# Decoder block: half of the next query ahead of the norm's transposes, values copied by ScalarE, and two additions moved into the attentions

## The chip, the cores and the metric

One core of a Trainium2 chip runs the whole program. The metric is the device time in microseconds of one execution. TensorE (PE), VectorE (DVE), ScalarE (ACT), GpSimd (POOL) and the DMA queue that SyncE issues (SP) run side by side and wait for each other through semaphores.

## The reference

A post-norm decoder block on 4 batches of 1024 tokens of width 256, with 16 heads of width 16: a self attention with low-rank query, key and value and rotary terms, a cross attention on 154 context rows, and a mixture of 8 experts.

```python
ct_q = x @ Wd_q_w + Wd_q_b
qt_c = heads(ct_q @ Wu_q_w + Wu_q_b)
qt_r = heads(_rope(ct_q @ Wq_r_w + Wq_r_b, cos, sin))
query = qt_c + qt_r
ct_kv = x @ Wd_kv_w + Wd_kv_b
kt_c = heads(ct_kv @ Wu_k_w + Wu_k_b)
kt_r = heads(_rope(x @ Wk_r_w + Wk_r_b, cos, sin))
key = kt_c + kt_r
value = heads(ct_kv @ Wu_v_w + Wu_v_b)
...
x = _layernorm(x + attention(query, key, value) @ Wo_w + Wo_b)
x = _layernorm(x + cross_attention(x, ctx))
x = _layernorm(x + experts(x))
```

## The kernel before

The batches run one after the other: self attention, a passage, cross attention, a second passage, and so on; the experts of all batches come at the end. The order on each engine is written out by hand, and semaphores join the engines. An attention has two kinds of score products. The maxima (L1582 in the self attention, L1573 and L1576 in the cross attention) are reduced by DVE (L1122, L1117) to one negative maximum per row. POOL splits that into three bf16 parts (`split_max`, L780 to L786), PE turns it (L1624), ACT copies it (L966) and SP loads it as three more rows of the query stack (L571). The transposed scores (L1640, L1646, L1657) then go through ACT's exponential (L958) and are multiplied with the values (L1674, L1678). Heads go in 8 groups of two. In the cross attention a group has 4 units of maxima; groups 0 to 3 read the query stack in `qxs` (semaphore `s_qx[0]`), groups 4 to 7 the one in `qst` (`s_qx[1]`). Five groups of maxima run before the first transposed score. A turn of group g stands in PE's order after the maxima of group g+1, so group g+2 waits for POOL's split of group g.

float32 accuracy is kept by splitting queries and keys into three bf16 parts, and a stack of 96 rows holds six products of parts. That is done in pieces of 128x512. Piece (b, i) is of batch b: i of 0 to 3 is the query (half i // 2 of the tokens, two pieces each), 4 to 7 the key, 8 the context's key, 9 to 12 the cross query, where 9 and 10 make the stack in `qxs` and 11 and 12 the one in `qst`. A piece goes: product on PE (one matmul of 512 float32 columns shows as two records); for a query or key the rotary step `roped` on DVE, two pieces at a time (L1070 and L1073, L1078 and L1079, and L1083, which writes `full`); for a cross query ACT's bias (L918, writes `full`). Then ACT's first part (L904), POOL's difference (L762), ACT's second part (L925), POOL's third (L769). ACT and POOL work one piece ahead: the second part of a piece stands behind the first part of the next one. SP stores the three parts of a piece to DRAM (L541, `store_piece`), and when all of a stack are stored (`stored`) loads them back six times (L566, `load_stack`: 6 DMAs of 256 KB). `full` and `rest` are two buffers each in `pT`; the parts have six slots, four in `kst` and two (`lent`) in `pT`.

In the passage from self to cross attention of batch b (`rest_of_batch`), PE makes the output projection (L1773), the latents of batch b+1 (L1549 with wdq and wdkv, taken by ACT at L932), the turns of the normalised x (L1541), the four cross queries `qx`, the query and key products of b+1 (L1793, L1796, L1549 with wkr) and its values (L1803). DVE normalises (L1173), does four rotary steps and adds the bias to the values (L1186). POOL adds the bias of the cross attention's output to the residual (L826) ahead of the pieces. PSUM has 8 banks, given out in turn: a product waits until the one eight places before it is taken.

Of the kernel before, what the change touches and what calls it, by code (L numbers as in the profile page):

```python
# [26 lines left out]
ALU = mybir.AluOpType  # L27
# [34 lines left out]
OPERANDS = [("q", "D")] * 8 + [("k", "D")] * 8 + [("v", "D")] * 4  # L62
CONTEXT = [("kx", "A"), ("vx", "D"), ("vxr", "D")]
FRONT = LATENTS + OPERANDS + CONTEXT
OUT_SELF = [("o", "D")] * T + [("oT", "DA"[n % 2]) for n in range(4)] + [("y", "D")] * 4
INTO_CROSS = [("x1T", "A")] * 4 + [("qx", "A")] * 4
# [54 lines left out]
PIECES = 13  # L121
RING = 6


def slot(i):
    return (i - (i > 8)) % RING


def stored_upto(ring, i):

    return len([n for n in range(i) if n != 8 and slot(n) == ring])
# [131 lines left out]
def decoder_block(nc, a, out):  # L263
    ctx = ExitStack()
    with ctx:
# [89 lines left out]
        parts_at = [part[:, i, :, :] for i in range(RING - 2)] + [lent[:, i, :, :] for i in range(2)]  # L355
# [92 lines left out]
        s_xb = sem("residual_ready")  # L448
        s_p1 = sem("part1_ready")
# [42 lines left out]
        def parts_of(i):  # L492
            return [part_x[:, k, :] if i == 8 else parts_at[slot(i)][:, k, :] for k in range(3)]
# [5 lines left out]
        def _(sp):  # L499
# [37 lines left out]
            def store_piece(b, i, dst, cols):  # L537

                sp.wait_ge(s_p4, b * PIECES + i + 1)
                for k in range(3):  # L540
                    sp.dma_start(dst[k], parts_at[slot(i)][:, k, 0:cols]).then_inc(s_pw[slot(i)], 16)  # L541

            def store_context(b):

                wait_apart(sp, s_p4, b * PIECES + 9)
# [5 lines left out]
            def stored(b, i):  # L551

                wait_apart(sp, *[w for r in range(RING) for w in (
                    s_pw[r], 48 * (b * stored_upto(r, PIECES) + stored_upto(r, i + 1)) + START)])

# [20 lines left out]
            def store_front(b, pieces):  # L576
                for i in pieces:
                    store_piece(b, i, rows_of(q_parts if i < 4 else k_parts, i % 2, i % 4 // 2), N)

            def load_keys(b, thirds):  # L580
                if 0 in thirds:
                    stored(b, 7)
# [30 lines left out]
            def rest_of_batch(b, more):  # L613
# [4 lines left out]
                def store_cross(pieces):  # L618
                    for i in pieces:
                        mc, half = (i - 9) // 2, (i - 9) % 2  # L620
                        store_piece(b, i, [qx_parts[k, mc * P:(mc + 1) * P, half * N:(half + 1) * N]
                                           for k in range(3)], N)

                def load_cross(mc):
                    stored(b, 10 + 2 * mc)
                    load_stack(heads_of(qst, 1) if mc else qxs[:, :, :], qx_parts, mc, 0, s_qx[mc])

                if more:
                    store_cross(range(9, 13))
                    load_cross(0)  # L630

                    wait_apart(sp, s_ql[0], b * 96 + 96, s_ql[1], b * 96 + 96, s_kl[0], b * 96 + 96,
                               s_kl[1], b * 96 + 96)
                    store_front(b + 1, range(4))
                    load_cross(1)
                    stored(b + 1, 3)
                    load_stack(heads_of(qst, 0), q_parts, 0, 0, s_ql[0])
                    store_front(b + 1, range(4, 8))
                else:
                    store_cross(range(9, 11))  # L640
                    load_cross(0)
# [1368 lines left out]
```

## Time and profile before

| | |
|---|---|
| median of 3 runs | 1862.75 us (1860.33 to 1869.51) |
| the profiled execution | 1864.3 us, of which the span on the engines is 1862.4 us |
| granted clock of TensorE, mean | 0.931 |
| busy: PE, DVE, ACT, POOL | 1638.1 us, 1203.4 us, 888.1 us, 430.6 us |
| first self attention starts | 69.05 us |
| passages from self to cross attention (from the last value product's end to the first cross maxima) | about 287 to 351 us, 664 to 726 us, 1038 to 1102 us; of the last batch 1413 to 1463 us |
| the chain that ended last: PE, DVE, issue, ACT, DMA | 67%, 11%, 6%, 5%, 4% |

A timeline row has the start, the duration, the engine, the line, the operation with output and inputs, how many, and in brackets the idle time before it and what ended it. Rows "x4" that overlap in time are pipelined.

### The profile page before, as it was taken

Reading aid. Unit: us, or ns where it says so; the run is one execution under the profiler, and the core shown is the slowest. Engines: PE = TensorE matmul, PEld = TensorE weight load, DVE = VectorE, ACT = ScalarE, POOL = GpSimd, SP = SyncE. Lnnn points to the kernel's source line nnn. Section 1 sums busy time; section 2 is a strip of 40 time slices with the busy share of each in tenths; the row PEclk is TensorE's granted clock in tenths of the full one; section 3 lists DMA queues with packets and bytes.
Section 4 is the critical chain, followed back from the end, with each engine's and each line's share of the span. In section 5 each row is a group of like instructions: output and inputs, shape, how many; then the busy total and the mean of one; then the engine's idle time right before and its main releaser. Section 6 shows DMA issues by size and latency. Waiting matters only on the chain.

```text
span 1862.4 us, 27223 instructions
## 1 busy us (share of the span) xinstructions
PE 1638.1 (88%) x10046; PEld 814.2 (44%) x10046; DVE 1203.4 (65%) x2136; ACT 888.1 (48%) x1582; POOL 430.6 (23%) x543
## 2 busy tenths in 40 slices
PE   7499999798899997988999979889997698999993
PEld 3023325445233244452332445523324446888873
DVE  5577744865777759647777496477776634664443
ACT  2067774252677742526777425257774261111111
POOL 4300003501100025011000260110001401566663
PEclk9589999898899998988999989889999797999997
DMA  5800001823100017222000072220000413455594
GB/s 183 180 6 1 1 2 43 208 53 79 54 1 1 2 35 207 62 64 68 2 2 1 27 204 73 62 71 2 2 2 1 120 48 102 74 113 111 113 260 116
DMA packets 108256, 128.24 MB, mean 69 GB/s; under 512 B 17244, under 2 KB 81756, under 8 KB 108124
## 3 DMA queue, kind: packets, MB, share of 16 engines
q1 hardware_dynamic: 95836, 109.71, 21.3%
q0 software_dynamic: 12288, 16.79, 5.4%
q8 instruction: 80, 1.31, 0.3%
q14 instruction: 52, 0.43, 0.1%
HBM read 84.49 MB, written 40.79 MB: 67 GB/s over the span
## 4 chain that ended last, share of the span: by engine, by line
PE 67%; DVE 11%; issue 6%; ACT 5%; DMA 4%; POOL 2%; SPq 2%; POOLq 0%; ACTq 0%; DVEq 0%
PE banks L1674 13%; PE banks L1640 11%; PE banks L1582 10%; PE banks L1921 5%; PE banks L1934 4%; PE banks L1773 2%; PE banks L1573 2%; PE banks L1549 2%; PE banks L1576 2%; PE banks L1644 2%; PE banks L1624 2%; PE banks L1678 2%; PE banks L1684 2%; DVE z L1143 2%; PE banks L1831 2%
## 5 line engine op out<-in xcount | busy, mean ns | idle before, releaser
L958 ACT ACTIVATE pT<-banks 128x512 f32<-128x512 f32 x1184 | 645.1, 595 | 272.7 <-PE banks L1640 167.5
L1122 DVE TENSOR_REDUCE nmf<-banks 128x1 f32<-128x1024 f32 x512 | 606.0, 1221 | 183.3 <-PE banks L1582 181.9
L1640 PE MATMUL banks<-qst,kst 99*128 99x512 bf16 x1024 | 349.8, 389 | 18.8 <-DMA qst<-nmT 9.3
L1582 PE MATMUL banks<-kst,qst 96*128 96x512 bf16 x1024 | 328.0, 405 | 32.7 <-DMA kst<-k_parts 22.8
L1674 PE MATMUL banks<-pT,V 128*32 128x512 f32 x2048 | 274.5, 608 | 17.3 <-ACT oT L946 12.2
L1640 PEld LDWEIGHTS banks<-qst,kst 99*128 99x128 bf16 x1024 | 95.9, 97 | 312.6 <-ACT pT L958 187.0
L780 POOL CAST nmp<-nmf 128x16 bf16<-128x16 f32 x64 | 12.7, 198 | 833.4 <-issue 759.5
L1582 PEld LDWEIGHTS banks<-kst,qst 96*128 96x128 bf16 x1024 | 98.6, 100 | 148.9 <-DVE nmf L1122 36.8
L1117 DVE TENSOR_REDUCE nmf<-banks 128x4 f32<-128x616 f32 x128 | 99.9, 798 | 66.1 <-PE banks L1576 58.9
L1027 ACT ACTIVATE kst<-banks 128x512 f32<-128x512 f32 x64 | 38.2, 597 | 205.8 <-PE banks L1921 205.8
L966 ACT ACTIVATE nmT<-banks 6x1024 bf16<-6x1024 bf16 x64 | 64.8, 1013 | 130.3 <-PE banks L1624 129.1
L819 POOL DMA_INDIRECT acc_rows<-kst,tok_s x64 | 103.1, 1611 | 47.6 <-DMA acc_rows<-kst,tok_s 17.9
L1573 PE MATMUL banks<-maskb,identb 128*128 128x308 bf16 x256 | 81.4, 330 | 31.9 <-DVE V L1186 25.8
L1674 PEld LDWEIGHTS banks<-pT,V 128*32 128x32 f32 x2048 | 41.3, 108 | 126.9 <-ACT pT L958 126.0
L793 POOL TENSOR_TENSOR rstd<-ve,mhalf 128x4 f32<-128x4 f32 x16 | 16.3, 1020 | 330.0 <-DVE ve L1167 330.0
L1434 DVE TENSOR_SCALAR kst<-banks,gate 128x256 f32<-128x256 f32 x64 | 28.0, 479 | 95.1 <-PE banks L1934 95.1
L810 POOL DMA_INDIRECT kst<-x_rows,tok_g x64 | 65.4, 1021 | 70.8 <-issue 49.7
L1141 DVE RECIPROCAL rz<-banks 128x16 f32<-128x16 f32 x64 | 15.9, 249 | 101.7 <-PE banks L1757 101.7
L889 ACT ACTIVATE xT<-banks 128x512 f32<-128x512 f32 x40 | 22.7, 598 | 94.6 <-PE banks L1528 54.9
L1921 PE MATMUL banks<-kst,qst 128*128 128x256 f32 x256 | 60.3, 391 | 0.0
L1934 PE MATMUL banks<-qst,kst 128*128 128x256 f32 x256 | 58.4, 381 | 0.0
L1921 PE MATMUL banks<-kst,qxs 128*128 128x256 f32 x256 | 58.0, 379 | 0.3 <-issue 0.3
(200 smaller groups left out, 2296.9 us busy)
## 6 DMA issues: line engine op xcount, KB each, us to landing
qst<-q_parts SPq DMA_DIRECT2D x48, 256.0 KB, 6.3
kst<-k_parts SPq DMA_DIRECT2D x48, 256.0 KB, 4.4
qst<-in_w SPq DMA_DIRECT2D x16, 512.0 KB, 5.2
qxs<-in_w SPq DMA_DIRECT2D x16, 512.0 KB, 5.0
q_parts<-kst SPq DMA_DIRECT2D x48, 128.0 KB, 2.4
qxs<-qx_parts SPq DMA_DIRECT2D x24, 256.0 KB, 5.2
qst<-qx_parts SPq DMA_DIRECT2D x24, 256.0 KB
kst<-in_xT SPq DMA_DIRECT2D x4, 1024.0 KB, 5.0
```

The source lines that it names most:

```text
L810: pool.indirect_dma_start(xg[k][:, j, :], None, x2_rows[0:(EARLY if n < EARLY * E else B) * S, :], bass.IndirectOffsetOnAxis(tok_g[q % 2][ ...
L819: pool.indirect_dma_start(acc_rows, bass.IndirectOffsetOnAxis(tok_s[q % 2][:, k, j:j + 1], 0), yg[k][:, j, :], None, compute_op=ALU.add).t ...
L958: act.activation(pT[:, n % RING_P, :], PS[:, banks[what, n], :], ACT.Exp, scale=scale).then_inc(s_ex, 1)
L966: act.activation(nmT[:, m % 2, :], PS[0:3 * G, banks[what, n], :].bitcast(BF16), ACT.Copy).then_inc(s_ne, 1)
L1117: dve.tensor_reduce(nmf[:, m % 2, j, 4 * u:4 * u + 4].rearrange("p (a t) -> p a t", a=2), scores[:, :, 0:2 * SK].rearrange("p a (t k) -> p ...
L1122: dve.tensor_reduce(nmf[:, m % 2, j, t:t + 1], scores.rearrange("p a n -> p (a n)"), AX.X, ALU.max, negate=True).then_inc(s_smu, 1)
L1573: pe.matmul(ps[:, 0:2 * SK], identb[:, :], maskb[:, t0:t0 + 2, 0:SK], start=True, stop=False, skip_group_check=True)
L1582: ins = pe.matmul(pair[:, half, :], qst[0:KQ, h, t * P:(t + 1) * P], kst[0:KQ, h, half * N:(half + 1) * N], start=True, stop=True)
L1640: ins = pe.matmul(ps, kst[0:KM, head, kc * P:(kc + 1) * P], qst[0:KM, head, cols], start=True, stop=True)
L1674: ins = pe.matmul(av[V32 * j:V32 * (j + 1), :], Vf[:, kc, (g * G + j // HALVES) * VD:(g * G + j // HALVES) * VD + V32], pT[:, n % RING_P, ...
L1921: ins = pe.matmul(PS[:, 2 + 2 * k + f // 2, (f % 2) * CAP:(f % 2 + 1) * CAP], we1[w % WEIGHTS][:, c, f * P:(f + 1) * P], xgT[k][:, c, :], ...
L1934: ins = pe.matmul(PS[:, 6 + k, j * D:(j + 1) * D], hT[k][:, f, j * P:(j + 1) * P], we2[w % WEIGHTS][:, f, :], start=(f == 0), stop=(f == F ...
```

## The change

In the passages between two batches PE multiplies the first half of batch b+1's query ahead of the turns of the normalised x, then two of the four cross queries, then the rest of the query, the keys and values, and last the other two cross queries. The pieces get one numbering over the whole program (`PIECES`, `NUMBER`), in the order (b+1,0), (b+1,1), (b,9), (b,10), (b+1,2) to (b+1,7), (b,11), (b,12), (b+1,8); ACT, POOL and SP follow it. SP loads the stack in `qxs` behind (b,10), the first query stack of b+1 behind (b+1,5) and the second cross stack behind (b,12). The values are copied by ACT without their bias (new `values`, 4 ACTIVATE), just ahead of piece (b+1,6), and POOL adds the bias to all of them in one instruction behind the split of cross group 3 (`bias_values`, semaphore `s_vb`, for which the first product with the values waits). At the start of the program the values stand behind piece (0,7) on ACT, and the bias behind piece (0,8) on POOL. POOL's addition to the residual (`after_layernorm`) moves from ahead of the pieces to behind the split of cross group 1, in the last batch too; `mask_bias` and `residual` of b+1 move behind the splits of self groups 1 and 2.

```diff
-OPERANDS = [("q", "D")] * 8 + [("k", "D")] * 8 + [("v", "D")] * 4
+HALF_Q = [("q", "D")] * 4
+KEYS = [("k", "D")] * 8
+VALUES = [("v", "A")] * 4
...
-EACH = Plan(OUT_SELF + LATENTS + INTO_CROSS + OPERANDS, OUT_CROSS + CONTEXT + ROUTING)
-LAST = Plan(OUT_SELF + INTO_CROSS, OUT_CROSS + ROUTING)
+EACH = Plan(OUT_SELF + LATENTS + HALF_Q + TURNED + HALF_X + HALF_Q + KEYS + VALUES + HALF_X,
+            OUT_CROSS + CONTEXT + ROUTING)
+LAST = Plan(OUT_SELF + TURNED + HALF_X * 2, OUT_CROSS + ROUTING)
...
+def pieces_between(b):
+
+    if b < 0:
+        return [(0, i) for i in range(9)]
+    if b == B - 1:
+        return [(b, i) for i in range(9, 13)]
+    return ([(b + 1, 0), (b + 1, 1), (b, 9), (b, 10)] + [(b + 1, i) for i in range(2, 8)]
+            + [(b, 11), (b, 12), (b + 1, 8)])
...
+                for piece in pieces_between(b):
+                    if piece[1] == 8:
+                        continue
+                    store_piece(piece)
+                    if piece == (b, 10):
+                        stored(piece)
+                        load_stack(qxs[:, :, :], qx_parts, 0, 0, s_qx[0])
+                    elif piece == (b + 1, 5):
+                        stored((b + 1, 3))
+                        load_stack(heads_of(qst, 0), q_parts, 0, 0, s_ql[0])
+                    elif piece == (b, 12):
+                        stored(piece)
+                        load_stack(heads_of(qst, 1), qx_parts, 1, 0, s_qx[1])
...
+            def bias_values(b):
+
+                at = Place(EACH, b - 1) if b else Place(FIRST)
+                pool.wait_ge(s_eva, at.taken("A", at.nth("v", 3) + 1))
+                pool.tensor_tensor(V[:, :, :, 0:HD], V[:, :, :, 0:HD],
+                                   brow[:, 0, :].rearrange("p (t h d) -> p t h d", t=1, d=HD)
+                                   .to_broadcast([P, T, H, HD]), ALU.add).then_inc(s_vb, 1)
+
+            def after_layernorm(b):
+
+                pool.wait_ge(s_ln, b * 2 * T + T)
+                pool.tensor_tensor(xb[:, :, :], z[:, :, :], brow[:, 3:4, :].to_broadcast([P, T, D]),
+                                   ALU.add).then_inc(s_xb, 1)
...
+                split([piece for piece in pieces_between(b) if piece[1] != 8])
+                cross, own = SM_CROSS // NG, SM_SELF // NG
+                split_max(b, SM_SELF, NG, cross, range(1))
                 if not more:
 
                     pool.wait_ge(s_x2, EARLY * 32 + START)
                     pool.wait_ge(s_tk, 1)
                     for n in range(SLOTS):
                         gather(n)
-                    split_max(b, SM_SELF, NG, SM_CROSS // NG, range(1, NG))
+                split_max(b, SM_SELF, NG, cross, range(1, 2))
+                after_layernorm(b)
+                split_max(b, SM_SELF, NG, cross, range(2, 4))
                 if more:
-                    split_max(b + 1, 0, 0, SM_SELF // NG, range(1))
+                    bias_values(b + 1)
+                split_max(b, SM_SELF, NG, cross, range(4, NG))
...
+            def values(at):
+                for k in range(4):
+                    idx = at.nth("v", k)
+                    taken_before(at, idx)
+                    act.activation(V[:, 2 * k:2 * k + 2, :, 0:HD],
+                                   PS[:, at.bank(idx), :].rearrange("p (t h d) -> p t h d", t=2, d=HD),
+                                   ACT.Copy).then_inc(s_eva, 1)
...
+                        if pieces[step] == values_ahead_of:
+                            values(at)
+                        part1(at, pieces[step])
+                    if step > 0:
+                        part2(pieces[step - 1])
...
+            parts(Place(FIRST), pieces_between(-1)[:8])
+            act.wait_ge(s_ms, 1)
+            values(Place(FIRST))
+            parts(Place(FIRST), [(0, 8)])
...
+                    operands(at, "q", 0)
                 turn_normalised(at, b, "x1T", 0)
                 for i in range(4):
                     if i < 2:
-                        taken_upto(at, at.nth("x1T", 2 * i + 1) + 1)
+                        wait_taken(at, "A", at.nth("x1T", 2 * i + 1) + 1)
+                    elif i == 2 and more:
+                        operands(at, "q", 1)
+                        operands(at, "k", 0)
+                        operands(at, "k", 1)
+                        values(at)
```

How the order of the instructions moves, at the three places that matter most. PE in the passage after self attention 0; `ident,z` are the turns of the normalised x, `xT,w` the cross queries, `kst,wqr` and `kst,wuq` a half of the query, `kst,wkr` with `ctkv,wuk` a half of the keys, `wuv,ctkv` the values. Before:

```order
367 L1549 MATMUL banks<-kst,wdkv 128x512 x4
368 L1541 MATMUL banks<-ident,z 128x128 x16
369 L1549 MATMUL banks<-xT,w 128x512 x8
370 L1793 MATMUL banks<-kst,wqr 128x512 x2
371 L1796 MATMUL banks<-kst,wuq 128x512 x2
372 L1793 MATMUL banks<-kst,wqr 128x512 x2
373 L1796 MATMUL banks<-kst,wuq 128x512 x2
374 L1549 MATMUL banks<-kst,wkr 128x512 x4
375 L1796 MATMUL banks<-ctkv,wuk 128x512 x2
376 L1549 MATMUL banks<-kst,wkr 128x512 x4
377 L1796 MATMUL banks<-ctkv,wuk 128x512 x2
378 L1803 MATMUL banks<-wuv,ctkv 128x256 x8
379 L1573 MATMUL banks<-maskb,identb 128x308
```

After:

```order
367 L1577 MATMUL banks<-kst,wdkv 128x512 x4
368 L1825 MATMUL banks<-kst,wqr 128x512 x2
369 L1828 MATMUL banks<-kst,wuq 128x512 x2
370 L1569 MATMUL banks<-ident,z 128x128 x16
371 L1577 MATMUL banks<-xT,w 128x512 x4
372 L1825 MATMUL banks<-kst,wqr 128x512 x2
373 L1828 MATMUL banks<-kst,wuq 128x512 x2
374 L1577 MATMUL banks<-kst,wkr 128x512 x4
375 L1828 MATMUL banks<-ctkv,wuk 128x512 x2
376 L1577 MATMUL banks<-kst,wkr 128x512 x4
377 L1828 MATMUL banks<-ctkv,wuk 128x512 x2
378 L1835 MATMUL banks<-wuv,ctkv 128x256 x8
379 L1577 MATMUL banks<-xT,w 128x512 x4
380 L1601 MATMUL banks<-maskb,identb 128x308
```

Half a query stands ahead of the turns now, and half of the cross queries behind the values, right ahead of the first cross maxima.

SP's queue in the same passage; `qx_parts` takes cross query pieces, `q_parts` and `k_parts` query and key pieces (three DMAs each), and a load into `qxs` or `qst` is a stack of six DMAs. Before:

```order
34 L541 DMA qx_parts<-kst 128x512 x6
35 L541 DMA qx_parts<-pT 128x512 x6
36 L566 DMA qxs<-qx_parts 16x8x1024 x6
37 L541 DMA q_parts<-kst 16x8x512 x12
38 L566 DMA qst<-qx_parts 16x8x1024 x6
39 L566 DMA qst<-q_parts 16x8x1024 x6
40 L541 DMA k_parts<-pT 16x8x512 x6
41 L541 DMA k_parts<-kst 16x8x512 x6
42 L571 DMA qxs<-nmT 3x2x1024
```

After:

```order
34 L566 DMA q_parts<-pT 16x8x512 x6
35 L566 DMA qx_parts<-kst 128x512 x6
36 L591 DMA qxs<-qx_parts 16x8x1024 x6
37 L566 DMA q_parts<-kst 16x8x512 x6
38 L566 DMA k_parts<-pT 16x8x512 x6
39 L591 DMA qst<-q_parts 16x8x1024 x6
40 L566 DMA k_parts<-kst 16x8x512 x6
41 L566 DMA qx_parts<-kst 128x512 x6
42 L591 DMA qst<-qx_parts 16x8x1024 x6
43 L596 DMA qxs<-nmT 3x2x1024
```

The load `qst<-qx_parts` stood ahead of `qst<-q_parts` and of all stores of keys; it stands behind them and behind the last two cross pieces now.

ACT at the start of the program, from the second-last key piece to the context piece (`part_x`). Before:

```order
16 L904 ACTIVATE kst<-pT 128x512
17 L925 ACTIVATE kst<-pT 128x512
18 L914 ACTIVATE pT<-banks,bcol 128x154 x2
19 L904 ACTIVATE part_x<-pT 128x308
20 L925 ACTIVATE kst<-pT 128x512
21 L925 ACTIVATE part_x<-pT 128x308
```

After:

```order
16 L932 ACTIVATE kst<-pT 128x512
17 L954 ACTIVATE kst<-pT 128x512 x2
18 L960 ACTIVATE V<-banks 128x2x16x16 x4
19 L943 ACTIVATE pT<-banks,bcol 128x154 x2
20 L932 ACTIVATE part_x<-pT 128x308
21 L954 ACTIVATE part_x<-pT 128x308
```

The four copies into `V` and both bias steps of the context stand between the last key piece and its follower on POOL.

## Rows read from the trace of the kernel before

**Rows 1.** Timeline of PE, self to cross passage of batch 0: start, us.
```profile
311.14 1.91 PE L1541 MATMUL banks<-ident,z 128*128 128x128 f32 x16
...
313.06 7.13 PE L1549 MATMUL banks<-xT,w 128*128 128x512 f32 x16
...
320.03 1.88 PE L1793 MATMUL banks<-kst,wqr 128*128 128x512 f32 x4
...
351.27 0.44 PE L1573 MATMUL banks<-maskb,identb 128*128 128x308 bf16 x1 [8.59 <-DVE V L1186]
...
367.07 0.30 PE L1573 MATMUL banks<-maskb,identb 128*128 128x308 bf16 x1
```

**Rows 2.** Timeline of DVE, the same passage and the maxima.
```profile
321.15 0.75 DVE L1070 SCALAR_TENSOR_TENSOR kst<-banks,bcol,cosT 128x512 f32<-128x512 f32 x1 [10.73 <-PE banks L1793]
...
326.42 1.41 DVE L1083 SCALAR_TENSOR_TENSOR pT<-banks,bcol,kst 128x512 f32<-128x512 f32 x2
...
339.88 1.41 DVE L1083 SCALAR_TENSOR_TENSOR pT<-banks,bcol,kst 128x512 f32<-128x512 f32 x2
...
347.15 1.41 DVE L1083 SCALAR_TENSOR_TENSOR pT<-banks,bcol,kst 128x512 f32<-128x512 f32 x2
348.48 2.73 DVE L1186 TENSOR_TENSOR V<-banks,brow 128x256 f32<-128x256 f32 x8
...
352.58 0.80 DVE L1117 TENSOR_REDUCE nmf<-banks 128x4 f32<-128x616 f32 x1 [1.37 <-PE banks L1576]
...
357.21 3.11 DVE L1117 TENSOR_REDUCE nmf<-banks 128x4 f32<-128x616 f32 x4 [0.70 <-PE banks L1576]
...
367.89 3.11 DVE L1117 TENSOR_REDUCE nmf<-banks 128x4 f32<-128x616 f32 x4 [0.45 <-PE banks L1576]
```

**Rows 3.** Timeline of ACT, the same passage.
```profile
311.34 0.69 ACT L932 ACTIVATE ctkv<-banks,bcol 128x512 f32<-128x512 f32 x1 [1.03 <-PE banks L1549]
```

**Rows 4.** Timeline of POOL, the same passage.
```profile
310.51 4.53 POOL L826 TENSOR_TENSOR xb<-z,brow 128x2048 f32<-128x2048 f32 x1 [1.50 <-DVE z L1173]
...
349.85 1.16 POOL L769 TENSOR_TENSOR pT<-pT 128x512 bf16<-128x512 f32 x1
...
352.25 2.27 POOL L769 TENSOR_TENSOR kst<-pT,kst 128x512 bf16<-128x512 f32 x2
```

**Rows 5.** Timeline of SP's queue, the same passage.
```profile
345.81 3.79 SPq L566 DMA_DIRECT2D qst<-qx_parts  x6
...
357.52 3.83 SPq L541 DMA_DIRECT2D k_parts<-kst  x6
...
366.89 1.24 SPq L566 DMA_DIRECT2D kst<-k_parts  x2
```

**Rows 6.** Timeline of SP and of PE at the start of the program.
```profile
44.75 4.33 SPq L566 DMA_DIRECT2D qst<-q_parts  x6
...
59.45 7.65 SPq L566 DMA_DIRECT2D kst<-k_parts  x12
...
69.05 1.87 PE L1582 MATMUL banks<-kst,qst 96*128 96x512 bf16 x4 [22.78 <-DMA kst<-k_parts]
```

**Rows 7.** Windows of 2 us: PE, PEld, DVE, ACT, POOL busy, PEclk, DMA share, GB/s.
```profile
346.00:348.00 2.00, 0.00 (x0) 0.00 (x0) 1.96 (x3) 0.06 (x1) 0.57 (x1) 0.65 0.67 153
348.00:350.00 2.00, 0.00 (x0) 0.00 (x0) 2.00 (x6) 1.68 (x4) 1.26 (x2) 0.50 1.10 250
...
356.00:358.00 2.00, 1.39 (x11) 0.82 (x9) 1.30 (x3) 0.00 (x0) 0.84 (x4) 0.79 1.06 224
```

**Rows 8.** Timeline of DVE and SP in the last batch's passage.
```profile
1436.77 3.96 DVE L1281 TENSOR_TENSOR kst<-prob,thr_all 128x192 bf16<-128x192 f32 x1
1440.77 0.36 DVE L1282 TENSOR_TENSOR kst<-prob,thr_all 128x192 bf16<-128x192 f32 x1
...
1446.21 3.67 SPq L541 DMA_DIRECT2D qx_parts<-kst  x6
1451.50 3.99 SPq L566 DMA_DIRECT2D qxs<-qx_parts  x6
```

More of the change, by code:

```diff
@@ L118, in piece, with stored_upto @@
         return self.nth(name, n)
-PIECES = 13
 RING = 6
[L125 to L131, printed above, removed]
+LENT = 2
+def pieces_between(b):
[5 more added lines that the diff above has]
+            + [(b, 11), (b, 12), (b + 1, 8)])
+PIECES = [piece for b in range(-1, B) for piece in pieces_between(b)]
+NUMBER = {piece: n for n, piece in enumerate(PIECES)}
+STORED = [piece for piece in PIECES if piece[1] != 8]
+SLOT = {piece: n % RING for n, piece in enumerate(STORED)}
+def stored_upto(slot, number):
+    return len([piece for piece in PIECES[:number] if SLOT.get(piece) == slot])
 SM_SELF, SM_CROSS = H * T, H * 2
@@ L617, in rest_of_batch @@
                 wait_apart(sp, s_qx[0], b * 96, s_qx[1], b * 96, s_ql[1], b * 96 + 96)
[L618 to L626, printed above, removed]
-                if more:
[L629 to L641, printed above, removed]
-                    store_cross(range(11, 13))
-                    load_cross(1)
+                if more:
+                    wait_apart(sp, s_ql[0], b * 96 + 96, s_kl[0], b * 96 + 96, s_kl[1], b * 96 + 96)
+                for piece in pieces_between(b):
[11 more added lines that the diff above has]
+                        load_stack(heads_of(qst, 1), qx_parts, 1, 0, s_qx[1])
                 load_minus_max(b, NG, cross_rows(0))
@@ L674, in rest_of_batch @@
                     self_attention(b + 1)
-            store_front(0, range(4))
-            stored(0, 3)
-            load_stack(heads_of(qst, 0), q_parts, 0, 0, s_ql[0])
-            store_front(0, range(4, 8))
+            for i in range(8):
+                store_piece((0, i))
+                if i == 3:
+                    stored((0, i))
+                    load_stack(heads_of(qst, 0), q_parts, 0, 0, s_ql[0])
             load_keys(0, range(6))
@@ L1587, in cross_q, with attention @@
                 return qxs[:, h, :] if h < H // 2 else qst[:, h, :]
-            def attention(b, n0, u0, g0, order, cross):
+            def attention(b, n0, u0, g0, order, cross, at=None):
                 per = (ST_CROSS if cross else ST_SELF) // NG
@@ L1670, in attention @@
                             pe.wait_ge(s_pe2, 1 + START)
+                        if n == 0 and not cross:
+                            pe.wait_ge(s_vb, b + 1)
                         av = PS[:, AV_BANK, :]
@@ L1856, in rest_of_batch @@
                         rank_chosen(EARLY * E, EARLY * TURNS + 2)
-                if more:
-                    for name in "qk":
-                        for half in range(HALVES):
-                            operands(at, name, half)
-                    values(at)
                 taken_upto(at, at.nth("v" if more else "qx", 3) + 1)
```

174 lines of the change are left out of this document (82 added, 92 removed).

## Prediction

> **What bounds the kernel now.** I read the page first: PE is busy 88% of the span and has 67% of the chain that ended last. So what can be won is time in which PE waits. The timeline of PE shows it in each passage from self to cross attention. The reader is to see that PE has its products done and then stands idle for 8.59 us until DVE has added the bias to the values, and starts the cross maxima at 351.27 [rows 1]. The timeline of DVE says why [rows 2]: it idles 10.73 us until PE's first query product comes at 321.15, then does four rotary steps in a row (to 327.83, about 334, 341.29 and 348.56) and the values (2.73 us). Next I read on past the start of the cross attention, because a stage that starts earlier gains only if its next input comes earlier too. DVE takes a group of maxima every 3.56 us (357.21 to 367.89 are three groups) [rows 2], and PE begins group 4, the first that reads the second cross stack, at 367.07 without a wait [rows 1]. That stack's load was issued at 345.81 [rows 5], 21 us ahead.
>
> **PE and DVE, passages of batches 0 to 2.** The half query needs both halves of ctkv, which ACT finishes at 311.34 + 0.69 = 312.0 [rows 3], where PE went on at 311.14 [rows 1]: 1.0 us lost. A record of a 512-column matmul takes 7.13 / 16 = 0.43 us or so [rows 1], so half a query (8 records) is 3.4 us: 312.1 to 315.5. The turns (1.9) end at 317.5, two cross queries (3.4) at 320.9, and the second half of the query begins there, 0.9 to 1.0 later than the first does now (320.03). DVE's first rotary step falls into its idle time and costs nothing. The three others start at about 322.1 instead of 321.15. Three steps take 20.1 us (321.15 to 341.29) or 20.7 (327.83 to 348.56) [rows 2]; I take 20.7, as they run beside POOL's pieces. The last keys are ready at F = 342.8, 5.8 earlier than 348.56. The values leave DVE (2.73); ACT's four copies at up to 0.69 each [rows 3] lie in front of piece (b+1,6), for which it waits longer. PE's last two cross queries end by 341. So DVE and PE would let the cross attention start at 343, 8 us earlier.
>
> **POOL.** Its addition of 4.53 us [rows 4] leaves the head of the passage, where it hid behind PE, and stands behind group 1; the one on the values has the same size (bound: once to twice 4.53 because of its short runs) and stands behind group 3. Behind F, POOL now has four pieces to finish instead of two: it ended 354.52 - 348.56 = 5.96 us after F [rows 4], two more pieces at 1.16 x 2 each give 10.6, so 353.4. Split 0 follows at 354.6, and group 2 waits for it instead of starting at 343 + 7.1 = 350.1. Group 3 ends near 362. All of this is hidden if group 4 has to wait for something later, and it has.
>
> **SP, the term that decides.** The second cross stack now comes last. Piece (b+1,5) is done 351.01 - 348.56 = 2.45 us behind F [rows 4], since its second part stands behind the first part of (b+1,6). Three issues of 0.64 (3.83 / 6 [rows 5]) follow, so the load of the query stack is issued at 342.8 + 2.45 + 2.1 = 347.3. Behind it come four pieces (two of keys, two of the cross query), the wait that they are stored, and only then the load of the cross stack. The start of the program has nearly this sequence [rows 6]: query stack issued at 44.75, four pieces stored, the next load free at 59.45: 14.7 us. The passage gives 21.1 us for two stacks and four pieces (345.81 to 366.89) [rows 5], with the DMA share at 1.1 and 250 GB/s [rows 7]; a stack is 1.57 MB, 7 us at some 220 GB/s, which leaves 14.1. I take 14.4: 361.7. From there a stack needs 9.6 us until PE starts on it (59.45 to 69.05 [rows 6]; bounds 8 to 10, since there six more DMAs were behind it). Group 4 starts at 371.3 instead of 367.07: 4.2 us **later**, though the stage before it began 8 us earlier.
>
> **The clock.** PE is then idle from about 362 to 371. In the idle time of today the granted clock falls from 1.00 through 0.65 to 0.50 and is back at 0.79 in the window 356 to 358 [rows 7], so 5.3 us after 351.27 the level is 2.4 GHz again. The four units at the 1.2 GHz level take 357.21 - 352.58 = 4.63 against 3.56 us and the first comes 1.3 us behind PE's start against 0.8; in the new place the transposed scores of the first units are slow as well. I take 2.0 (bounds 0, if the idle time is short, and 2.7, half of 5.3). Today this price is paid at 351.27 too, in a stretch whose gain is now hidden.
>
> Sum of a passage: 4.2 + 2.0 = 6.2, times three 18.6.
>
> **The start.** The four copies and the context's steps stand ahead of POOL's third part of (0,7): 4 x 0.69 and about 1.2 more, up to 4 us. The DMA queue is behind anyway there (14.7 us for work that POOL delivers sooner), so I take 0.8, bounds 0 to 4. SP's and PE's first wait (L1582 at 69.05) moves by it [rows 6].
>
> **The last batch.** POOL's addition held up DVE: the same kind of instruction took 3.96 us beside it and 0.36 behind it [rows 8]. That frees 3.6 us in DVE's chain, but the first cross stack is issued at 1451.50 [rows 8] and lands 9.6 later at 1461, against maxima at about 1462. So -1.0, bounds -3.6 and 0. `mask_bias` and `residual` of the next batch go behind splits of self groups, where POOL has nothing else to do until the next group of 16 maxima is reduced: 0.
>
> **The sum** against the profiled execution: 1864.3 + 18.6 + 0.8 - 1.0 = 1882.7. It lay 1.55 above the median of the runs, 1862.75, so 1881.
>
> A rule that bears on SP's term is in the Trainium skill, page "DMA: Bandwidth & Descriptors", section "Queues, rings and completion order": each DMA engine takes its descriptors in ring order. By that rule a store waits behind a stack that was issued ahead of it, and this speaks against the change. The trace agrees: with an idle queue SP goes on 1.6 us after the last store's issue (1446.21 + 3.67 to 1451.50) [rows 8], behind a stack 5.5 us after (357.52 + 3.83 to 366.89) [rows 5].
>
> **Rivals.**
> *The stores are not held up by the load.* Then SP goes on at its pace of issue: 347.3 + 3.8 + 3.8 + 2.6 + 1.6 = 359.1, the stack is there at 8 to 9.6 behind that, 367.5 to 368.7. A passage costs 0.5 to 1.6 and some 1 for the clock: with 2 each, 1864.3 + 6 - 0.2 - 1.55 = 1868.5, no change that can be told. For it: nobody waited closely on that queue but in two places. Against it: those two rows of 5.5 and 14.7.
> *The stack comes in time* (faster). The point from which it decides is PE's group 4 at 367.07. If the stack is ready when group 3 is done, near 362.5, a passage gains 4.6 and keeps the clock: 1864.3 - 13.7 - 0.2 - 1.55 = 1848.8. For it: F is earlier by a whole rotary step and the first stack is early enough. Against it: from F to PE's start the shortest way is 10.6 (POOL) + 1.5 (issue) + 1.6 + 8 = 21.7, so 364.5, even with an empty DMA queue.
> *The queue is worse than taken*: bounds of 15 and 10 us and 2.7 for the clock give 8 a passage, 1888.
>
> **How the numbers follow.** About 0.5%, 9 us, is what a measurement of this kernel can tell from no change. Slower as summed, 0.72 (own range 1873 to 1890); the stores not held up or the clock not lost, within 0.5%, 0.16; the stack in time, 0.12. The likeliest gives 1881. The range of 8 in 10 takes in the second case: 1863 to 1890.
>
> **What would show it.** In the changed profile the cross maxima should start near 343 to 344, and PE should then stand 7 to 10 us at group 4, released by the load of `qst` from `qx_parts`; SP should issue that load near 362; DVE should have no adds to V; the clock should be at 0.5 when group 4 starts. The forecast is wrong if group 4 starts before 367 counted like this, that is less than 79 us behind the last product of the self attention's end at 287; if the second stack's load is issued before 357; or if PE waits for group 2 or 3 longer than for group 4, which would make POOL the bound.

## The result

The changed kernel takes 1885.27 us (median of 4 runs, 1882.76 to 1889.27), the kernel before 1861.93 beside it (1860.33 to 1869.51): a ratio of 1.0118, 95% interval 1.01 to 1.0135. The change makes the kernel slower, by 1.2% or some 23 us. Its profiled execution took 1883.76 us, with a span of 1881.5 us, against 1864.3 before.

The page of the changed kernel, span and busy times, and the row of the cross maxima; the last line is the same row in the page of the kernel before:

```profile
span 1881.5 us, 27223 instructions
...
PE 1644.2 (87%) x10046; PEld 819.8 (44%) x10046; DVE 1185.4 (63%) x2104; ACT 895.5 (48%) x1598; POOL 446.1 (24%) x547
...
L1158 DVE TENSOR_REDUCE nmf<-banks 128x4 f32<-128x616 f32 x128 | 100.2, 798 | 114.1 <-PE banks L1604 110.4
...
L1117 DVE TENSOR_REDUCE nmf<-banks 128x4 f32<-128x616 f32 x128 | 99.9, 798 | 66.1 <-PE banks L1576 58.9
```

DVE has 18 us less to do (1203.4 before) and PE's work is the same to 6 us, yet the kernel is 19 us longer. The last two rows say where: DVE waits 114.1 us ahead of the cross maxima, where it waited 66.1 before.

PE in the passage of batch 0, the answer to [rows 1]; line 1601 is the start of a cross maximum, line 1654 turns the minus-maxima of a group:

```profile
310.52 1.98 PE L1825 MATMUL banks<-kst,wqr 128*128 128x512 f32 x4 [0.78 <-ACT ctkv L969]
...
342.74 0.30 PE L1601 MATMUL banks<-maskb,identb 128*128 128x308 bf16 x1 [2.59 <-DMA qxs<-qx_parts]
...
353.53 1.01 PE L1654 MATMUL banks<-identb,nmp 128*6 128x128 bf16 x8 [3.57 <-POOL nmp L795]
...
361.79 0.61 PE L1654 MATMUL banks<-identb,nmp 128*6 128x128 bf16 x8
370.62 0.41 PE L1601 MATMUL banks<-maskb,identb 128*128 128x308 bf16 x1 [8.22 <-issue]
```

The half query stands ahead of the turns at 310.52. The maxima start at 342.74, 8.5 us before [rows 1]. Then PE waits for POOL's split (3.57) and 8.22 us for group 4, whose first input is in the second cross stack. Group 4 starts at 370.62 instead of 367.07. For these 8.22 us the profile names no engine ("issue"), but they end with the stack: in e1, e2, e4 and e7 below, where the landing of each DMA is on record, PE starts group 4 in all twelve passages 0.09 us behind the landing of the stack's last DMA. What it waited for stands in SP's rows of the same passage, the answer to [rows 5]:

```profile
346.07 3.79 SPq L591 DMA_DIRECT2D qst<-q_parts  x6
349.90 3.89 SPq L566 DMA_DIRECT2D k_parts<-kst  x6
353.84 3.05 SPq L566 DMA_DIRECT2D qx_parts<-kst  x6
359.41 3.80 SPq L591 DMA_DIRECT2D qst<-qx_parts  x6
```

The query stack goes out at 346.07, then the stores of four pieces, and only at 359.41 the second cross stack. Of the 13.34 us from 346.07 to 359.41, SP is busy with issuing for 10.8, the 3.79 for the query stack among them; it is through with the stores at 356.9 and waits 2.5 us for them to land. The windows of 1 us show the DMA engines meanwhile (PE, PEld, DVE, ACT, POOL busy, PEclk, DMA share, GB/s):

```profile
353.40:354.40 1.00, 0.87 (x8) 0.76 (x8) 0.00 (x0) 0.00 (x0) 0.71 (x4) 0.50 1.04 198
...
355.40:356.40 1.00, 1.00 (x9) 0.79 (x6) 0.61 (x1) 0.20 (x1) 1.00 (x1) 0.50 1.10 381
...
358.40:359.40 1.00, 1.00 (x15) 0.81 (x13) 0.74 (x1) 0.53 (x1) 0.67 (x2) 1.00 0.31 105
359.40:360.40 1.00, 0.62 (x8) 0.35 (x5) 0.81 (x2) 0.49 (x1) 0.70 (x4) 1.00 0.00 0
```

Only from about 354.5 do the engines move at 380 GB/s, which is the stores' rate here; before, at 198 to 246 GB/s in the windows from 351.4 to 354.4, they moved the query stack. The stores are done at 358.7, and the DMA engines stand idle until the new load reaches them at about 360.8.

To compare all passages, the table below counts from the first row of the self attention's output (line 1141 before, 1182 after) and gives means over batches 0 to 2: F, the end of DVE's last rotary step; group 4's first product with the second stack; and the end, the same row of the cross attention's output. "Behind" is the end less group 4. Each ratio is against runs of the kernel before on the same chip, whose medians lay between 1860.59 and 1863.51.

| | F | group 4 | end | behind | time, us | ratio and interval |
|---|---|---|---|---|---|---|
| before | 59.46 | 77.94 | 139.35 | 61.41 | 1861.93 | |
| changed | 54.07 | 83.27 | 146.69 | 63.42 | 1885.27 | 1.0118 (1.01 to 1.0135) |
| e1 | 54.05 | 77.98 | 145.26 | 67.27 | 1881.51 | 1.0115 (1.0071 to 1.0159) |
| e2 | 59.52 | 80.33 | 143.12 | 62.79 | 1875.75 | 1.0079 (1.0053 to 1.0105) |
| e3 | 55.75 | 72.34 | 142.16 | 69.82 | 1869.56 | 1.0033 (1.0015 to 1.005) |
| e4 | 54.71 | 78.26 | 141.76 | 63.50 | 1871.27 | 1.006 (1.0036 to 1.0084) |
| e5 | 55.13 | 71.38 | 134.43 | 63.04 | 1851.81 | 0.9931 (0.9918 to 0.9945) |
| e6 | 54.56 | 83.50 | 144.91 | 61.41 | 1882.18 | 1.0081 (1.005 to 1.0113) |
| e7 | 54.06 | 82.94 | 146.13 | 63.19 | 1884.21 | 1.0111 (1.0083 to 1.0139) |
| e8 | 55.33 | 73.50 | 136.62 | 63.12 | 1856.38 | 0.9957 (0.9942 to 0.9973) |
| e9 | 56.70 | 72.62 | 135.29 | 62.67 | 1852.05 | 0.9935 (0.9914 to 0.9955) |
| e10 | 54.51 | 78.20 | 140.56 | 62.35 | 1869.29 | 1.004 (1.0026 to 1.0054) |

Three passages cost 3 x 7.34 = 22.0 us. The last batch's passage and cross attention take 0.4 more (126.37 and 126.74), the three stages from cross to the end of the next self attention 1.3 less (707.2 and 705.9), what lies behind the last cross attention 2.0 less, and the start 0.1 less: 19.1, the difference of the two spans.

### The profile page after: what moved, and what is told of

The parts are those of the page before. It is cut to its first block and busy times, and to the rows that moved or that the text cites. A ratio compares the mean times of both kernels' runs of the same rounds, so it can differ in the third digit from the quotient of the medians.

```text
span 1881.5 us, 27223 instructions
## 1 busy us (share of the span) xinstructions
PE 1644.2 (87%) x10046; PEld 819.8 (44%) x10046; DVE 1185.4 (63%) x2104; ACT 895.5 (48%) x1598; POOL 446.1 (24%) x547
## 5 line engine op out<-in xcount | busy, mean ns | idle before, releaser
L1158 DVE TENSOR_REDUCE nmf<-banks 128x4 f32<-128x616 f32 x128 | 100.2, 798 | 114.1 <-PE banks L1604 110.4
L1654 PE MATMUL banks<-identb,nmp 128*6 128x128 bf16 x512 | 43.6, 235 | 17.9 <-POOL nmp L795 17.9
```

The lines of the kernel that those rows point to most:

```text
L1158: dve.tensor_reduce(nmf[:, m % 2, j, 4 * u:4 * u + 4].rearrange("p (a t) -> p a t", a=2), scores[:, :, 0:2 * SK].rearrange("p a (t k) -> p ...
```

## Experiments

### e1: the query stack's load behind the second cross stack

```
-  elif piece == (b + 1, 5):
-      stored((b + 1, 3))
-      load_stack(heads_of(qst, 0), q_parts, 0, 0, s_ql[0])
...
   load_minus_max(b, NG, cross_rows(0))
+  if more:
+      load_stack(heads_of(qst, 0), q_parts, 0, 0, s_ql[0])
```

> The changed kernel with one edit: in the passages the load of the next query stack is issued behind the load of the second cross stack and the first minus-maxima, instead of ahead of four pieces' stores. Theory (that load holds up the stores behind it): SP issues the second cross stack about 5 us earlier than the changed kernel does, near 354.5 to 356 in batch 0 instead of 359.4, since POOL is done with the last piece at 352.3; group 4 starts at 364 to 366.5 instead of 370.6, a passage is 4 to 7 us shorter, and the kernel takes 1865 to 1873. Rival (the stores go at their own pace and the stack is late because the last pieces are): the issue moves by less than 1 us, time 1882 to 1887.

Measured: 1881.51 us, a miss by the time and a hit by the place. SP and PE, e1, batch 0:

```profile
351.87 2.77 SPq L566 DMA_DIRECT2D qx_parts<-kst  x6
356.15 3.80 SPq L591 DMA_DIRECT2D qst<-qx_parts  x6
360.81 3.81 SPq L591 DMA_DIRECT2D qst<-q_parts  x6
...
365.74 0.29 PE L1600 MATMUL banks<-maskb,identb 128*128 128x308 bf16 x1 [2.11 <-issue]
376.65 0.61 PE L1673 MATMUL banks<-identb,maskb 128*128 128x128 bf16 x4 [3.86 <-ACT nmT L1002]
```

Group 4 starts 5.3 us earlier (77.98 against 83.27), so the place of the query stack does cost what it was said to cost, and the expectation's rival (less than 1 us) falls. How it costs is another question. In batch 0 the cross stack is issued 3.26 us earlier. Of these, 2.25 are SP's own time: its last store is issued at 354.64 instead of 356.89, since it has no six DMAs of 3.79 us to issue first. The other 1.0 is the wait for the stores to land, 1.51 us here and 2.52 in the changed kernel. A further 1.6 us lie behind the issue (9.59 us to PE's start, against 11.21). But PE now waits 3.86 us at the scores of group 1, since the minus-maxima of that group, 12 KB, stand behind the query stack in the queue. The 1.57 MB that was in front of one transfer was now in front of another, and "behind" grew from 63.4 to 67.3.

### e2: the kernel before, with the second cross stack loaded last

```
   store_front(b + 1, range(4))
-  load_cross(1)
   stored(b + 1, 3)
   load_stack(heads_of(qst, 0), q_parts, 0, 0, s_ql[0])
   store_front(b + 1, range(4, 8))
+  load_cross(1)
```

> The kernel before with one edit: SP issues the load of the second cross stack behind the next query stack and the four key pieces, as the changed kernel does; PE, DVE, ACT and POOL are as before. Theory (the place of that load in the queue is what costs): it is issued at about 362 in batch 0, group 4 starts at 371 to 373 instead of 367.07, and with the lower clock behind the wait a passage costs 5.5 to 8 us: 1879 to 1886, all that the change costs, without any of its other edits. Rival (what costs is the late production of the last two cross pieces on PE, ACT and POOL): 1862 to 1868.

Measured: 1875.75 us, ratio 1.0079. One line moved in SP's order, with nothing else of the change, costs 3.8 us a passage and 13 to 14 us in all, more than half of what the change costs. It is below the 5.5 to 8 expected, because group 4 starts at 80.33 and not at 82 to 84: here the cross pieces are long stored, and only key pieces stand between the two stacks. Nor does SP wait for anything in two of the three passages: in batch 0 it issues without a pause from 344.66, the query stack, to 356.49, the cross stack. What delays the cross stack's issue here is SP's own time. The rest of the change, which also makes the last two cross pieces late, costs 3.6 us a passage more, net of what it wins.

### e3 and e4: the last cross pieces into POOL's gaps

Both take this order of pieces; PE's products go along with it (one cross query ahead of the keys, one behind them). e3 has e1's order of SP, e4 the changed kernel's.

```
-  return ([(b + 1, 0), (b + 1, 1), (b, 9), (b, 10)] + [(b + 1, i) for i in range(2, 8)]
-          + [(b, 11), (b, 12), (b + 1, 8)])
+  return ([(b + 1, 0), (b + 1, 1), (b, 9), (b, 10), (b + 1, 2), (b + 1, 3), (b, 11), (b + 1, 4), (b + 1, 5),
+           (b, 12), (b + 1, 6), (b + 1, 7), (b + 1, 8)])
```

> e1 with a further edit: piece (b,11) is made and stored behind (b+1,3), piece (b,12) behind (b+1,5), in gaps of POOL, with their products on PE moved along; so the second cross stack is loaded before the last two key pieces are ready. Theory (only the lateness of that stack hides the 8 us that the half query ahead wins): it is issued near 344, lands near 354, POOL is done near 348, the maxima run through from 343 and group 4 starts at 357 to 359 without a wait; a passage is 7 to 10 us shorter than in the kernel before: 1833 to 1842. Rival (something else is late at once, POOL with the splits or the first minus-maxima): above 1850.

> The pieces and products as in e3, but the load of the next query stack where the changed kernel has it, behind piece (b+1,5). Theory (queue in order): the second cross stack is issued some 5 to 9 us later than in e3 and starts group 4 at 359 to 364: 1838 to 1855. Rival (the queue's order is worth nothing once the pieces come early): the same time as e3 within 2 us.

Measured: 1869.56 us for e3, a miss; 1871.27 for e4, above its range too. In e3 group 4 starts at 72.34, 10.9 us before the changed kernel's (2 to 4 us later than expected, since the first maxima start only at 56.4: in batch 0 they wait for the first cross stack, in batches 1 and 2 for DVE's last rotary step, F), and most of it is lost again. SP and PE, e3, batch 0:

```profile
352.81 3.80 SPq L591 DMA_DIRECT2D qst<-qx_parts  x6
361.37 4.75 SPq L591 DMA_DIRECT2D qst<-q_parts  x6
...
374.94 0.61 PE L1673 MATMUL banks<-identb,maskb 128*128 128x128 bf16 x4 [6.31 <-ACT nmT L1002]
```

The same wait as in e1, now 6.31 us, since PE is there earlier. `nmT` has two halves; ACT may fill the third group's only when the first has been loaded, and the second group's load stands behind the query stack. e4, where the query stack is out of the way by then, has 1.08 us of it, but starts group 4 5.9 us later than e3. It is as fast as e3 within 2 us, as the rival had it, but not for the rival's reason: the query stack costs e4 5.9 us ahead of group 4, and e3 6.3 us behind it (69.82 against 63.50).

e4 is also the run that shows stores held up by a load in front of them. SP, e4, batch 0:

```profile
347.81 3.79 SPq L591 DMA_DIRECT2D qst<-q_parts  x6
351.64 1.61 SPq L566 DMA_DIRECT2D qx_parts<-kst  x3
357.93 4.35 SPq L591 DMA_DIRECT2D qst<-qx_parts  x6
```

The last three stores stand right behind the query stack, and SP waits 4.68 us for them to land; in e3, without the stack in front, it waits 1.46.

The Trainium skill, page "DMA: Bandwidth & Descriptors", section "Queues, rings and completion order", says that descriptors on each DMA engine are consumed in ring order. The traces agree, down to a transfer of 12 KB. In e1 the minus-maxima of group 1 are issued at 367.25, behind the query stack, and ACT goes on at 375.58, 8.3 us later; in e5 below, without the stack in front, it is 3.6 us (363.50 to 367.06). The 3.86 and 6.31 us of PE are the price of this and of SP's time for the six DMAs.

### e5: the query stack in portions

e3, with the six DMAs of the query stack behind the minus-maxima of groups 3 and 4, where SP had little to do; the first maxima that read them start 98.3 us behind the start of the passage of batch 0, the last two of the six are issued at 86.0.

```
   load_minus_max(b, NG, cross_rows(0))
-  if more:
-      load_stack(heads_of(qst, 0), q_parts, 0, 0, s_ql[0])
   for g in range(1, NG):
-      if more and g < NG - 1:
-          load_keys(b + 1, range(g - 1, g))
+      if more and g in (4, 5):
+          load_stack(heads_of(qst, 0), q_parts, 0, 0, s_ql[0], range(4) if g == 4 else range(4, 6))
+      if more and g != 4:
+          load_keys(b + 1, range(g - 1 - (g > 4), g - (g > 4)))
```

> e3 with the next query stack's six DMAs taken from behind the first minus-maxima and put behind the fourth (four of them) and the fifth (two), and the key loads for the heads 8 to 15 one group later. Theory (in e3 the query stack in front of the minus-maxima of group 1 is what PE waited 6.31 us for, since only two sets of them fit in SBUF): that wait is under 1.5 us, group 4 starts as in e3 at 71 to 73 us behind the start of the passage, the passage ends 62 to 65 us later, and a passage is 5 to 8 us shorter than in e3: 1845 to 1855, faster than the kernel before by 0.4 to 0.9%. Rival (the queue has too much to move in any order, so that another load is late by as much, at the latest the next self attention's first maxima): 1863 to 1870.

Measured: 1851.81 us, ratio 0.9931 (0.9918 to 0.9945): faster than the kernel before by 0.7%, and 33 us faster than the changed kernel with the same instructions on every engine. The rows of e5, batch 0:

```profile
350.96 3.79 SPq L591 DMA_DIRECT2D qst<-qx_parts  x6
368.89 2.50 SPq L591 DMA_DIRECT2D qst<-q_parts  x4
373.87 1.80 SPq L591 DMA_DIRECT2D qst<-q_parts  x2
...
344.52 0.29 PE L1600 MATMUL banks<-maskb,identb 128*128 128x308 bf16 x1 [3.64 <-DMA qxs<-qx_parts]
368.13 0.40 PE L1673 MATMUL banks<-identb,maskb 128*128 128x128 bf16 x4 [1.07 <-ACT nmT L1002]
```

Of the 6.31 us 1.07 is left; group 4 does not wait; a passage takes 134.4 us against 139.35 before.

### e6: PE kept busy while it waits

```
+  if g and b < B - 1:
+      for _ in range(48):
+          pe.matmul(PS[:, AV_BANK, 0:2 * SK], identb[:, :], maskb[:, 0:2, 0:SK],
+                    start=True, stop=True, skip_group_check=True)
   pe.wait_ge(s_qx[g * G // 8], b * 96 + 96)
```

> The changed kernel, with 48 more matmuls of 308 columns (some 6.5 us at the 2.4 GHz level) into a bank that nobody reads, ahead of PE's wait for the second cross stack in the passages of batches 0 to 2. They write nothing that is used. Theory (PE's idle time lowers the granted clock, and what follows the wait is slow for it): group 4 starts when it did, at 82 to 84 us behind the start of the passage, the windows behind it show a clock of 1.00 or nearly, and from there to the end of the passage it takes 61.3 us as in the kernel before, not 63.5: 1.5 to 2.2 us a passage, 1878 to 1881. Rival (the slow stretch behind the wait has another cause, as the loads beside it): 1884 to 1887 with the clock as it was.

Two windows of the changed kernel and two of e6, each from group 4 on:

```profile
372.00:374.00 2.00, 2.00 (x13) 1.30 (x12) 1.51 (x2) 0.00 (x0) 0.00 (x0) 0.50 1.02 219
374.00:376.00 2.00, 2.00 (x14) 1.35 (x13) 1.60 (x2) 0.11 (x1) 0.04 (x1) 0.50 0.39 119
```

```profile
374.00:376.00 2.00, 1.38 (x13) 1.03 (x14) 0.99 (x2) 0.00 (x0) 0.00 (x0) 1.00 1.07 225
376.00:378.00 2.00, 2.00 (x24) 1.43 (x23) 1.90 (x3) 0.24 (x1) 0.00 (x0) 1.00 1.00 242
```

Group 4 starts when it did (83.5), the clock stays at its 2.4 GHz level, and "behind" is 61.40 to 61.42 us in the three passages, what it is in the kernel before. So the 2.0 us of a passage are the clock, and PE's idle time ahead of it is their cause. The loads beside it are no cause; they run in e6 too. The time, 1882.18, lies between the two ranges that were expected. The profiled execution was the longest of its four (1887.95): the stages behind the passages took 6.2 us more than in the changed kernel (712.2 and 705.9), which the last section comes to.

### e7: the key loads a group later

```
-  if more and g < NG - 1:
-      load_keys(b + 1, range(g - 1, g))
+  if more and g > 1:
+      load_keys(b + 1, range(g - 2, g - 1))
```

> The changed kernel with the six key loads of the passage one group later each: the first behind the minus-maxima of group 1 instead of ahead of them. In the changed kernel group 4 starts 11.2 us behind the issue of the second cross stack's load; in e1, e2 and e4 and for the first cross stack in e5 it was 9.6 to 9.8. Theory (the key loads, issued 1 to 5 us behind that load, take part of the DMA engines from it): it becomes 9.5 to 10, group 4 starts 1.3 us earlier in each passage, 1879 to 1884. Rival (something else, as the stores in front): it stays at 11.0 to 11.4, and the time at 1883 to 1887.

Measured: 1884.21 us. From the issue of the second cross stack to group 4's first product with it, it takes 10.8, 11.1 and 11.1 us, in the changed kernel 11.4, 11.3 and 11.4. The theory had 9.5 to 10 and falls: 0.3 to 0.6 us of this are the key loads behind it.

### e8: PE kept busy ahead of the first stack

e5 with 22 of e6's matmuls ahead of the wait for the first cross stack.

> e5 with 22 more matmuls of 308 columns (some 3 us) into a bank that nobody reads, ahead of PE's wait of 3.64 us for the first cross stack in the passages of batches 0 to 2; they write nothing that is used. Theory (as in e6: the idle time lowers the clock): the maxima of groups 0 and 1 run at a clock of 1.00 instead of 0.50, group 4 starts 1 to 2 us earlier than in e5, and the kernel takes 1845 to 1850. Rival (what is won there is waited for later, as POOL's splits of group 0 behind the pieces or the second stack set the time of groups 2 to 4): 1850 to 1854.

Measured: 1856.38 us, slower than e5. The row of the extra matmuls, batch 0:

```profile
342.11 3.04 PE L1591 MATMUL banks<-maskb,identb 128*128 128x308 bf16 x22 [2.69 <-issue]
```

The experiment did not do what it should. PE stood 2.69 us ahead of them. The profile names no engine for that, but in all three passages they begin 0.10 us behind F, the end of DVE's last rotary step, as the first maxima of e5 do in batches 1 and 2, where the profile names that step. So they began only 1 us before the stack was due in batch 0, and in the other two passages they covered no wait at all. The first maxima then came at 58.9 us into the passage on average instead of 55.7. In batch 0 the clock stayed at 1.00 in all windows from 344 to 354, where e5 has 0.50 from 346 to 352, and from the first maxima to group 4 it took 14.6 us instead of 15.7: 1.1 us back for 3.2 spent. Such work must end before what it covers, or it is itself the wait.

### e9: without the half query

```
-  EACH = Plan(OUT_SELF + LATENTS + HALF_Q + TURNED + HALF_X + HALF_Q + HALF_X[:1] + KEYS + HALF_X[:1] + VALUES,
+  EACH = Plan(OUT_SELF + LATENTS + TURNED + HALF_X + HALF_Q * 2 + HALF_X[:1] + KEYS + HALF_X[:1] + VALUES,
```

with pieces (b,9) and (b,10) ahead of (b+1,0) and (b+1,1), all else as e5.

> e5 without the half query ahead of the norm's turns: PE makes the latents, the turns, two cross queries and then the whole query, and pieces (b,9) and (b,10) come ahead of (b+1,0) and (b+1,1); all else as e5. Theory (with the queue out of the way the half query is worth what DVE's last rotary step comes earlier by): F is 59 to 60 us behind the start of the passage instead of 55 to 56.3, the first cross maxima start at 60.5 to 62, group 4 at 74.5 to 77, and a passage is 2.5 to 4.5 us longer than in e5: 1859 to 1866. Rival (POOL, the stack or the minus-maxima hide it, so that the half query is worth nothing even here): 1850 to 1855.

Measured: 1852.05 us, as fast as e5; a miss. F comes 1.6 us later (56.70), not 3 to 4: against the kernel before, PE does two cross queries fewer ahead of the query, so most of what the half query ahead wins is there without it. And in batch 0 the first cross stack is issued at 38.4 us instead of 46.9, since no query pieces stand ahead of its own, so the maxima start at nearly the same time there (56.5 and 56.8). In the other two they start 0.1 us behind F in both kernels, 2 us later in e9. A passage is 0.9 us longer (135.29 against 134.43), 2.6 us for the three. That is all the half query, the change's first part, is worth once the pieces stand in the right order, and the medians of these runs cannot tell it from nothing.

### e10: the changed kernel with e5's order of SP alone

> The changed kernel with SP's order of e5 alone: no load of the query stack ahead of the stores, its six DMAs behind the minus-maxima of groups 3 and 4; pieces, products and engines as in the changed kernel. In e1 the second cross stack was as early, but PE lost 3.86 us at the scores of group 1 for minus-maxima that were queued behind the query stack, and ended the passage at 143.3 to 146.5 us. Theory (that is all that e1 lost): group 4 starts at 77 to 78.5 us, no wait of over 1.5 us comes behind it, the passage ends at 138.5 to 141, as in the kernel before, and the time is 1860 to 1868. Rival (some other transfer is late in its place): 1874 to 1884, as e1.

Measured: 1869.29 us, 1.3 us above the range. All that e1 lost is back (no wait of over 1.5 us behind group 4, passages of 140.56 us), and it is still 0.4% slower than the kernel before: with the last cross pieces at the end of the row, group 4 starts at 78.2, and all that the other parts win ahead of it is waiting time, in batch 0 4.72 us for POOL's first split and 2.09 us for the stack. e10 against e5 is what the place of two pieces is worth, 17 us by the medians and 18 in the three passages.

## Why the prediction held, step by step

The forecast was 1881 us and the measured time 1885.27. The profiled execution lies nearer to the sum, 1883.76 against 1882.7; the other 3 us are where the profiled executions stand among their runs, 1.55 above the median before and 1.5 below it after.

**PE and DVE.** F was to come at 342.8, 5.8 earlier than before. It came at 341.55 in batch 0, but this passage had begun faster: from its first row to the latents it took 14.1 us against 15.6 before, a difference of clock that also shows in batch 1 before and in none of batches 1 and 2 after. As a mean of three F moved by 5.39. The half query cost PE 0.78 ahead of it for `ctkv`, where 1.0 was taken.

**POOL.** The first cross maxima came nearly as forecast (343 to 344; 342.74), POOL was done with the pieces 10.75 behind F (10.6 forecast), the first split came at once (352.25), and group 2 waited for it:

```profile
340.14 1.41 DVE L1124 SCALAR_TENSOR_TENSOR pT<-banks,bcol,kst 128x512 f32<-128x512 f32 x2
...
350.04 2.26 POOL L778 TENSOR_TENSOR kst<-pT,kst 128x512 bf16<-128x512 f32 x2
352.25 0.20 POOL L789 CAST nmp<-nmf 128x16 bf16<-128x16 f32 x1
...
363.91 4.15 POOL L814 TENSOR_TENSOR V<-V,brow 128x2048 f32<-128x2048 f32 x1
```

The addition on the values took 4.15 us, below the bound of "once to twice 4.53", and as the split of group 3 came ahead of it, it delayed nobody.

**SP, the deciding term.** From F to the query stack's issue: 4.5 forecast, 4.52 measured. From there to the cross stack's issue: 14.4 forecast, 13.34 measured. From there to PE: 9.6 forecast with bounds of 8 to 10, 11.2 measured, outside the bounds. The sum is 29.1 against 28.5, and with F earlier by 5.39 and not 5.8 group 4 moved by 5.3 us a passage, where 4.2 was taken. That the place in the queue costs this is shown by e1 and e2. Two errors nearly cancelled here, 1.1 us too long and 1.6 too short, and that is luck. Where the 11.2 comes from is open: by the first product it is 11.3 to 11.4 in the changed kernel's three passages and 9.6 to 10.4 in those of e1, e2, e4 and e10, and e7 leaves 0.3 to 0.6 us of it to the key loads.

The 14.4 rested on the reading that the stack holds up the stores. Its row from the start of the program, taken apart, is mostly SP's own time: in the kernel before SP issues until 57.55 and waits 1.9 us of the 14.7.

```profile
49.12 3.85 SPq L541 DMA_DIRECT2D k_parts<-pT  x6
53.01 4.54 SPq L541 DMA_DIRECT2D k_parts<-kst  x6
```

The 5.5 us of [rows 5] stood behind two stacks, issued at 345.81 and 349.85, and not behind one. In the changed kernel the wait is 2.5 us, 1.0 more than in e1. The rival's pace of issue gives 11.8 us for this step (3.8 + 3.8 + 2.6 + 1.6), so that the measured 13.34 lies 1.1 below the forecast and 1.5 above the rival: the two were closer than their chances say.

**The clock.** 2.0 forecast, 2.01 measured, and e6 takes exactly that away.

**The start.** +0.8 forecast, nothing measured: the first self maxima start at 69.14 against 69.05 [rows 6]. The stores were not waited for, as the lower bound had it.

**The last batch.** -1.0 forecast, +0.4 measured. The addition did leave DVE's way, 0.36 us instead of 3.96 [rows 8], and DVE then waited 3.39 for PE:

```profile
1457.41 0.36 DVE L1311 TENSOR_TENSOR kst<-prob,thr_all 128x192 bf16<-128x192 f32 x1
1464.70 0.18 DVE L1332 TENSOR_SCALAR kst<-banks 128x24 f32<-128x24 f32 x1 [3.39 <-PE banks L1733]
...
1458.37 5.64 PE L1577 MATMUL banks<-xT,w 128*128 128x512 f32 x8
...
1473.36 3.83 SPq L591 DMA_DIRECT2D qxs<-qx_parts  x6
1482.94 0.41 PE L1601 MATMUL banks<-maskb,identb 128*128 128x308 bf16 x1 [2.14 <-issue]
```

PE was slow, since its eight products took 5.64 us at a clock that stayed at 0.50 for the first 4 us (1458.4 to 1462.4), against 4.16 before, and the pieces, their stores and the first cross stack came 1.2 later. From that stack's issue to PE it was 9.58 us, as the step had it. With the same code e4 took 124.2 us for this stretch, e3 125.5 and the changed kernel 126.7: the term is smaller than its scatter.

**The sum**: 3 x 7.34 instead of 3 x 6.2, 0 instead of 0.8, 0.4 instead of -1.0, and 3.3 us less in the other stages, for which nothing was taken. The rivals: "not held up" falls with e4, where the stores do wait, and by its time, though SP's pace of issue, which it names, was most of the step (its 367.5 should be 367.1); "in time" did not happen here, and e3 and e5 show that it was to be had by another order of two pieces and one load; "worse than taken" (8 a passage; its terms add up to 1886.5, not 1888) is near to what was measured.

**What the prediction did not see** is the way out. It counted the query stack in front of the cross stack as a fact of the change. It did not ask when that stack is first read: 108.3 us into the passage of batch 0, 51 us after its issue. Using that slack is worth 16 of the 33 us between the changed kernel and e5 (e10); the other 17 are the place of the last two cross pieces.

## What to carry to other kernels

List for each transfer in a shared queue when it is issued and when it is first read, and put the one with the most slack last and in portions; here a load of 1.57 MB made late whatever stood behind it, large or small, by 3.79 us of SP's time for issuing it as much as by its time in the DMA engines. When a stage starts earlier, look for the input that it reads in its middle: if this doesn't come earlier too, the gain turns into waiting time, and on TensorE into a lower clock behind it. And an experiment that removes a wait can lay it on the next transfer, so read where the new wait is before the theory is given up.

## What was not expected of the hardware

**The rates of the two kinds of DMA.** Stores of pieces of 128 KB ran at 380 GB/s in the windows, loads of the stacks at about 200 to 250, with the DMA engines fully busy in both.

**The clock's return scatters.** Behind the cross attention, from the routing into the next self attention, PE stays at the 0.50 level for 24 us (24 to 48 us behind the first row of the cross attention's output), of which it is busy 18.3. In the changed kernel and in e5 the clock comes back at different points of the same sequence of instructions. These are the windows of the 8 us after that, batch 0, first of the changed kernel, then of e5:

```profile
482.41:490.41 8.00, 8.00 (x47) 2.23 (x45) 6.70 (x6) 5.92 (x11) 0.00 (x0) 0.97 0.00 0
```

```profile
471.72:479.72 8.00, 8.00 (x36) 2.21 (x35) 5.06 (x6) 4.83 (x9) 0.00 (x0) 0.77 0.00 0
```

0.97 and 0.77 are some 3 us at the lower level more, 1.6 us of work, and this stage takes 235.39 in the one and 237.20 in the other. In the twelve profiles these stages lie between 234.4 and 238.9 us; three of them make a scatter that hides a third of what was won in e5's passages (707.2 before, 712.5 in e5). What decides it was not tried.
